# Attention and MoE layer on eight cores: a bf16 input tile cast by the DMA, host-side token order, and the gating split in two

## The reference, cut to what matters

```python
def _L0_attn_ref(x, ...):                  # x: (16, 2048, 1024), SEG = 4, H = 8 heads
    ...                                    # tokens are grouped in segments of SEG = 4
    qk_in = xb @ proj_qk_w.T + proj_qk_b
    v_in = xb @ proj_v_w.T + proj_v_b
    q = (qk_in @ wq.T + bq); k = (qk_in @ wk.T + bk); v = (v_in @ wv.T + bv)
    scores = einsum('nqhd,nkhd->nhqk', q * scale, k)      # 4 x 4 in each segment
    scores = where(diag, finfo.min, scores)
    o = einsum('nhqk,nkhd->nqhd', softmax(scores), v)
    return o @ out_proj_w.T + out_proj_b

def _moe(x, Wg, W1, b1, W2, b2, W3, b3):   # 8 experts, top 2, DFF = 2048
    gout = xt @ Wg.T
    topv, topi = top_k(gout, 2); w = softmax(topv)
    comb = einsum('tke,tk->te', one_hot(topi, E), w)
    h = silu(xt @ W1.T + b1) * (xt @ W2.T + b2)           # every expert on every token
    eo = h @ W3.T + b3
    return einsum('eth,te->th', eo, comb)

x = layernorm(x + attn(x))
x = layernorm(x + moe(x))
```

## Time and profile before

| what | us |
|---|---|
| median of the timed runs (8247.62 to 8254.06) | 8250.84 |
| the profiled execution, its own time | 8323.93 |
| span of its slowest core (the other seven: 8187.3 to 8282.6) | 8322.4 |
| PE busy in that span | 6452.2 |
| VectorE busy | 2236.5 |
| attention phase, from the start to the first load of x1T | about 2131 |

### The profile page before, as it was taken

One profiled execution on the slowest core, in us unless ns is written; L12 is line 12 of the kernel. 1 busy time (PEld: TensorE's weight loads), 2 busy tenths in 40 slices (PEclk: granted clock), 3 DMA queues, 4 the chain that ended last, 5 costly groups with the idle time before them and its releaser, 6 DMA issues.

```text
span 8322.4 us, 79954 instructions; the slowest of 8 cores (8187.3 to 8322.4 us)
## 1 busy us (share of the span) xinstructions
PE 6452.2 (78%) x29024; PEld 2830.4 (34%) x29024; DVE 2236.5 (27%) x3944; ACT 1005.5 (12%) x1621; POOL 309.8 (4%) x591
## 2 busy tenths in 40 slices
PE   4543555335399999938999996699999939999995
PEld 1211222112144444413444442244444414444442
DVE  3334443444222222222222222222222222222111
ACT  0010000100111111111111111111111111111111
POOL 0000000000000000000000000000000000000000
PEclk8766777667699999969999998799999969999886
DMA  4000000000344344432444343234443324334331
GB/s 76 22 26 26 8 19 25 26 25 9 65 72 72 66 77 81 76 81 46 86 76 76 61 91 76 61 66 84 79 76 67 75 72 76 71 64 89 67 65 48
DMA packets 137641, 504.56 MB, mean 61 GB/s; under 512 B 45181, under 2 KB 45310, under 8 KB 127274
## 3 DMA queue, kind: packets, MB, share of 16 engines
q0 software_dynamic: 84080, 415.43, 27.2%
q1 hardware_dynamic: 53178, 84.02, 3.1%
HBM read 872.71 MB, written 41.94 MB: 110 GB/s over the span
## 4 chain that ended last, share of the span: by engine, by line
PE 73%; DVE 12%; DMA 8%; issue 4%; ACT 2%; DVEq 1%; SPq 0%; POOL 0%; ACTq 0%; POOLq 0%
PE pm L830 22%; PE pm L794 20%; PE pm L772 19%; PE pb L385 4%; DMA w2f<-w2T 3%; PE pb L341 3%; DVE ob L480 2%; PE pb L519 2%; DMA x1g<-x1f 2%; DVE Pb L420 1%; DVE Sb L427 1%; DMA X<-x 1%; DVE ob L477 1%; DMA x1T<-x1t 1%; PE pb L394 1%
## 5 line engine op out<-in xcount | busy, mean ns | idle before, releaser
L772 PE MATMUL pm<-x1T,w1f 128*128 128x512 bf16 x8192 | 1969.4, 384 | 28.4 <-DMA w1f<-w1T 21.1
L794 PE MATMUL pm<-x1T,w2f 128*128 128x512 bf16 x8192 | 1962.1, 383 | 11.7 <-DMA w2f<-w2T 11.5
L830 PE MATMUL pm<-w3sb,hsb 128*128 128x512 bf16 x8192 | 1804.3, 384 | 45.0 <-DVE hsb L803 45.0
L803 DVE SCALAR_TENSOR_TENSOR hsb<-pm,b2c_s,su 128x512 bf16<-128x512 f32 x1024 | 769.0, 751 | 2879.6 <-PE pm L772 2550.0
L781 ACT ACTIVATE su<-pm,b1c_s 128x512 bf16<-128x512 f32 x1024 | 705.8, 689 | 4525.5 <-PE pm L772 4447.4
L830 PEld LDWEIGHTS pm<-w3sb,hsb 128*128 128x128 bf16 x8192 | 806.5, 99 | 1042.8 <-issue 161.6
L772 PEld LDWEIGHTS pm<-x1T,w1f 128*128 128x128 bf16 x8192 | 805.1, 99 | 1031.8 <-issue 138.0
L794 PEld LDWEIGHTS pm<-x1T,w2f 128*128 128x128 bf16 x8192 | 806.5, 99 | 1005.7 <-issue 104.0
L843 DVE SCALAR_TENSOR_TENSOR acc<-pm,comb,acc 128x512 f32<-128x512 f32 x512 | 384.4, 751 | 1462.7 <-PE pm L830 1459.7
L497 PE MATMUL trb<-idnb_s,obf 128*128 128x128 bf16 x256 | 32.4, 307 | 706.3 <-DVE obf L488 706.3
L161 POOL DMA_DIRECT2D w1f<-w1T x256 | 135.1, 528 | 6102.8 <-DVE hsb L803 3740.6
(11 more groups left out here) (94 smaller groups left out, 2177.9 us busy)
## 6 DMA issues: line engine op xcount, KB each, us to landing
w1f<-w1T POOLq DMA_DIRECT2D x256, 512.0 KB, 5.3
w2f<-w2T POOLq DMA_DIRECT2D x256, 512.0 KB, 7.3
w3sb<-w3T POOLq DMA_DIRECT2D x64, 2048.0 KB, 22.3
X<-x SPq DMA_DIRECT2D x8, 2048.0 KB, 9.8
x1f<-ob SPq DMA_DIRECT2D x32, 512.0 KB, 2.6
x1g<-x1f SPq DMA_DIRECT2D x32, 512.0 KB, 4.2
out<-outg SPq DMA_DIRECT2D x32, 512.0 KB, 2.9
x1t<-obf SPq DMA_DIRECT2D x32, 256.0 KB, 2.6
```

What stands on the lines that cost most here:

```text
L772: return t.matmul(gb[:, :], w1f[sl % 2][:, kt * 256 + off: kt * 256 + off + 128], x1T[:, kt * MCH + half * 512: kt * MCH + half * 512 + 51 ...
L794: return t.matmul(vb[:, :], w2f[sl % 2][:, kt * 256 + off: kt * 256 + off + 128], x1T[:, kt * MCH + half * 512: kt * MCH + half * 512 + 51 ...
L803: return v.scalar_tensor_tensor(hsb[:, f * MCH + half * 512: f * MCH + half * 512 + 512], vb[:, :], b2c[:, e * 16 + f: e * 16 + f + 1], su ...
L830: return t.matmul(bk[:, :], hsb[:, f * MCH + j * 128: f * MCH + j * 128 + 128], w3sb[:, f * D + half * 512: f * D + half * 512 + 512], sta ...
```

## The change

There are three edits, which come together.

1. The input is permuted on the host so that block i of a chunk is 128 rows in a row (`_vt_perm`), and the output is permuted back on the host; the store of `out` has contiguous rows. `X` (f32) and the two `Xc` tiles go. In their place `Xbf` (bf16, one for all chunks) is loaded on POOL's queue, with the cast done by the DMA, behind the six weights; it is free again after the chunk's last input transpose. The 256 casts of L306 go, and the transposes read `Xbf`.
2. The residual add reads `xres`, two f32 tiles of 128 tokens, each loaded on SP's queue ahead of its block's residual add.
3. The gating of a MoE chunk ends with `comb`. The transpose of `comb`, the copy `combT`, the bias matmuls and the copies into `acc` are a function of their own, `emit_gating_part2`, which is called once for each chunk, after expert 0's hidden stage and before its down-projection.

```diff
-    X = sba("X", [128, 4 * D], F32)
-    Xc = [sba(f"Xc{p}", [128, 128], BF16) for p in range(2)]
+    Xbf = sba("Xbf", [128, 4 * D], BF16)
+    xres = [sba(f"xres{p}", [128, D], F32) for p in range(2)]
...
-        xsrc = bass.AP(x_h.tensor, c * ACH * D, [[SEG * D, 128], [D, 4], [1, D]])
-        t_xl = dma("sync", X[:, :], xsrc, deps=take("X"), sem=ld_X)
+        xsrc = bass.AP(x_h.tensor, c * ACH * D, [[D, 128], [128 * D, 4], [1, D]])
+        t_xl = dma("gpsimd", Xbf[:, :], xsrc, deps=take("Xbf"), sem=ld_X)
...
-            bankdeps = take(bname) + (CONST if c == 0 and i == 0 else [])
+            bankdeps = [t_xl] + take(bname) + (CONST if c == 0 and i == 0 else [])
             ttr = None
             for dt in range(8):
-                t_c = vop(lambda v, s, i=i, dt=dt: v.tensor_copy(
-                    Xc[dt % 2][:, :],
-                    X[:, i * D + dt * 128: i * D + (dt + 1) * 128]),
-                    [t_xl] + take(f"Xc{dt % 2}"))
-
-                def f(t, s, dt=dt, bk=bk):
+                def f(t, s, i=i, dt=dt, bk=bk):
                     return t.transpose(bk[:, dt * 128:(dt + 1) * 128],
-                                       Xc[dt % 2][:, :], idnb[:, :])
-                ttr = top(f, [t_c] + bankdeps)
+                                       Xbf[:, i * D + dt * 128: i * D + (dt + 1) * 128],
+                                       idnb[:, :])
+                ttr = top(f, bankdeps)
                 bankdeps = []
-                use(f"Xc{dt % 2}", ttr)
+            last_tr = ttr
...
+        use("Xbf", last_tr)
...
+            vt0i = c * ACH + i * 128
+            t_xres = dma("sync", xres[par][:, :],
+                         bass.AP(x_h.tensor, vt0i * D, [[D, 128], [1, D]]),
+                         deps=take(f"xres{par}"), sem=ld_xr[par])
...
-                        X[:, i * D + half * 512: i * D + half * 512 + 512],
+                        xres[par][:, half * 512: half * 512 + 512],
                         bk2[:, :], OP.add)
-                tx = vop(fxr, [tmm] + take(f"xr{par}" if half == 0 else "_n"))
+                tx = vop(fxr, [tmm, t_xres]
+                         + take(f"xr{par}" if half == 0 else "_n"))
                 use(bname2, tx)
-                if i == 3 and half == 1:
-                    use("X", tx)
+                use(f"xres{par}", tx)
...
+        def emit_gating_part2():
+            for j in range(8):
+                def ftr(t, s, j=j):
+                    return t.transpose(pm[7][0:8, 0:128],
+                                       comb[:, j * 8:(j + 1) * 8], idnf[:, :])
+                ttr = top(ftr, [comb_tok[j]] + take("pm7"))
...
+            if e == 0:
+                emit_gating_part2()
+
             last_mm = None
             for j in range(8):
...
-            dst = bass.AP(out_h.tensor, (c_ * ACH + i_) * D,
-                          [[SEG * D, 128], [1, D]])
+            dst = bass.AP(out_h.tensor, vt0 * D, [[D, 128], [1, D]])
```

More of the change, by code:

```diff
@@ L133, in build_program @@
     ld_X = P.sem("ld_X")
+    ld_xr = [P.sem("ld_xr0"), P.sem("ld_xr1")]
     ld_x1T = P.sem("ld_x1T")
@@ L294, in build_program @@
     for c in range(N_ACH):
-        xsrc = bass.AP(x_h.tensor, c * ACH * D, [[SEG * D, 128], [D, 4], [1, D]])
-        t_xl = dma("sync", X[:, :], xsrc, deps=take("X"), sem=ld_X)
+        xsrc = bass.AP(x_h.tensor, c * ACH * D, [[D, 128], [128 * D, 4], [1, D]])
+        t_xl = dma("gpsimd", Xbf[:, :], xsrc, deps=take("Xbf"), sem=ld_X)
         xT_evacs = []
         xT_guard = take("xT")
+        last_tr = None
         for i in range(4):
@@ L325, in build_program @@
             xT_evacs.append(tev)
+        use("Xbf", last_tr)
         if DEBUG_TAPS and c == 0:
-            use("X", dma("sync", dbg["dbg_X"], X[:, :], deps=[t_xl], sem=st_dbgs["dbg_X"]))
             use("xT", dma("sync", dbg["dbg_xT"], xT[:, :], deps=xT_evacs,
@@ L532, in build_program, with fxr @@
                 use(f"oT{par}", tmm)
-                def fxr(v, s, par=par, half=half, bk2=bk2, i=i):
+                def fxr(v, s, par=par, half=half, bk2=bk2):
                     return v.tensor_tensor(
                         xr[par][:, half * 512: half * 512 + 512],
-                        X[:, i * D + half * 512: i * D + half * 512 + 512],
+                        xres[par][:, half * 512: half * 512 + 512],
                         bk2[:, :], OP.add)
-                tx = vop(fxr, [tmm] + take(f"xr{par}" if half == 0 else "_n"))
+                tx = vop(fxr, [tmm, t_xres]
+                         + take(f"xr{par}" if half == 0 else "_n"))
                 use(bname2, tx)
-                if i == 3 and half == 1:
-                    use("X", tx)
+                use(f"xres{par}", tx)
                 xr_parts.append(tx)
@@ L702, in build_program @@
             comb_tok[j] = t_cb
[L704 to L730, removed]
@@ new lines, in emit_gating_part2, with fce, fmm, fai @@
+        def emit_gating_part2():
[4 more added lines that the diff above has]
+                ttr = top(ftr, [comb_tok[j]] + take("pm7"))
+                def fce(v, s, j=j):
+                    return v.tensor_copy(combT[:, j * 128:(j + 1) * 128],
+                                         pm[7][0:8, 0:128])
+                t_ct = vop(fce, [ttr] + take(f"combTg{j}"))
+                use("pm7", t_ct)
+                for half in range(2):
+                    bn = f"pm{half}"
+                    def fmm(t, s, j=j, half=half):
+                        return t.matmul(pm[half][:, :],
+                                        combT[:, j * 128:(j + 1) * 128],
+                                        b3s[:, half * 512: half * 512 + 512],
+                                        start=True, stop=True)
+                    tmm2 = top(fmm, [t_ct] + take(bn))
+                    use(f"combTg{j}", tmm2)
+                    def fai(v, s, j=j, half=half):
+                        return v.tensor_copy(
+                            acc[:, j * D + half * 512: j * D + half * 512 + 512],
+                            pm[half][:, :])
+                    t_ai = vop(fai, [tmm2] + take(f"accg{j}{half}"))
+                    use(bn, t_ai)
+                    acc_tok[(j, half)] = t_ai
@@ L888, in build_program @@
             use(f"xr2{par}", t_o)
-            c_ = g // 4
-            i_ = g % 4
-            dst = bass.AP(out_h.tensor, (c_ * ACH + i_) * D,
-                          [[SEG * D, 128], [1, D]])
+            dst = bass.AP(out_h.tensor, vt0 * D, [[D, 128], [1, D]])
             t_st = dma("sync", dst, outg[par][:, :], deps=[t_o], sem=st_o[par])
@@ L975, in _host_prep, with _vt_perm @@
     }
+def _vt_perm():
+    p = np.empty(T, dtype=np.int64)
+    for c in range(N_ACH):
+        for i in range(4):
+            for n in range(128):
+                p[c * 512 + i * 128 + n] = c * 512 + 4 * n + i
+    return p
 def kernel(**inputs):
@@ L981 @@
     xs = x.reshape(N_CORES, 2 * 2048, D)
+    perm = _vt_perm()
     in_maps = []
@@ L984 @@
         m = dict(com)
-        m["x"] = np.ascontiguousarray(xs[c])
+        m["x"] = np.ascontiguousarray(xs[c][perm])
         in_maps.append(m)
@@ L988 @@
     res = run_bass_kernel_spmd(nc, in_maps, core_ids=list(range(N_CORES)))
-    out = np.concatenate([np.asarray(r["out"]).reshape(2, 2048, D)
-                          for r in res.results], axis=0)
-    return out.astype(np.float32)
+    outs = []
+    for r in res.results:
+        ov = np.asarray(r["out"])
+        oreal = np.empty_like(ov)
+        oreal[perm] = ov
+        outs.append(oreal.reshape(2, 2048, D))
+    return np.concatenate(outs, axis=0).astype(np.float32)
 if __name__ == "__main__":
```

## The result

The changed kernel takes 0.9818 of the time of the kernel before, with a 95% interval of 0.9798 to 0.9837: **1.8% less**. The forecast was 8101 us against 8250.84, a ratio of 0.982. The executions of the changed kernel that the ratio rests on took 8090 to 8134 us, all but one of them 8090 to 8100. What follows reads core 5 in both profiles. The first fence shows two cores of the changed kernel, with span and mean granted clock; the second is core 5 of the kernel before.

The account below looks back on a forecast made before the run. The chain was 73% PE, mostly MoE matmuls left unchanged; the change touches stretches where PE stands. Terms -162.4, +48.8 and -36 sum to -149.6 us, giving 8101 us from 8250.84, range 8080 to 8125, whole range 8055 to 8150.

Parts of the forecast that it names:

- the one from the sum to the chances: Turning the forecast time into chances: 0.24 for over 2% faster, 0.74 for within 2%, 0.02 for over 2% slower.
- The sum: Whole kernel: -162.4 at boundaries, +48.8 at the start, -36 for the gating split, together -149.6 us.
- the middle of expert 0: Between expert 0's hidden stage and down-projection: the moved gating rounds delay the down-projection, a loss of 21.8 us per MoE chunk.
- the cold restart: Expert 0's down-projection in each MoE chunk starts at the lower clock after the wait, costing 1.8 us.
- The boundary: Between attention chunks: copy to projection takes 5.1 us instead of 28.3, saving 23.2 at each of 7, 162.4 in all.
- The cold start that I left in: First projection matmuls of each attention chunk: a 2.2 us slow-clock cost assumed to stay, gain 0, at most 15 us.
- the rival that had it going: Cold start goes at 7 boundaries (15 us), Xbf lands at 84 (6), acc rounds faster (10): 181 us, 8070; chance 0.2.
- The first chunk: Program start: Xbf queues behind six weights, lands at 90.4, projection starts at 95.5; a loss of 48.8 us, between 42 and 60.
- xres: Residual add in attention: its 32 loads land in 4.2 us with 18.9 us of slack, cost 0.
- the rival that had it late: Residual add waits for xres: at a slow load's pace 822 us more, 8923 us; chance 0.02.
- The gating: MoE chunks: head gains 32.5 us, middle loses 21.8, cold start 1.8; net 8.9 each, 36 us for four.
- The rival that had it worthless: Gating split gives nothing if rounds in expert 0 take 3.9 us: 8137, or 8149 with Xbf landing at 102; chance 0.13.

Follow-up runs that it names:

- Xbf held back: The changed kernel with each next Xbf load held until the last copy of the chunk before; fastest time 8169 us, 77 us more than the changed kernel.
- the doubled transposes: The changed kernel with each of a chunk's 32 input transposes issued twice; fastest time 8099.38 us, 7 us more than the changed kernel, measured once.

## Why the prediction was right, and where it wasn't

**The step that failed is the one from the sum to the chances.** The prediction says "About 2% is what a measurement of this kernel can tell from no change", and so puts 0.74 on a time within 2%, as if 1.8% were no clear change. The record had the number against it: the timed runs of the kernel before, 8247.62 to 8254.06, lie within 0.08% of each other. The interval of the measurement is 0.4% wide (0.9798 to 0.9837), and no change, 1.0, stands far outside it. The sum said 150 us, and the bounds of its terms (137 for the boundaries, 60 for the first chunk, 0 for the gating split) leave a gain of 77 us even all together. What I should have drawn from it is that a gain was near certain, and only its being over or under 2% open; that stays open even now, for 0.98 lies inside the interval.

**The time and its direction were right**, with 1.8% forecast and 1.8% measured, and each mechanism of the sum was there. That the total came within 6 us of core 5's is in part luck: the boundaries gave 17 us more than their term, and the start, the middle of expert 0 and the cold restart together cost 12 us more than theirs.

- *The boundary.* The four rounds of 5.1 us are there, to 0.1 us. The term was the most mis-sized: 179.3 measured for 162.4. From the end of the last copy to the projection the seven boundaries took 203.1 us on core 5 before (29.0 each, where the one that I read had 28.3) and 35.1 after, a gain of 168.0. The wait for X is part of that: 103.0 less 24.0 at the start leaves 79.0, or 11.3 each, where I had 10.7. Another 6.4 us came from the projection that starts each of the seven stretches, which is the cold start, below. The last 5.0 lie in the four blocks of a chunk, and nothing here says why.
- *The cold start that I left in.* The step "I leave it in: the transposes of before do not clear it, and the new ones are denser but last only 5 us" failed. The projection's first matmuls gained 7.6 us over the 8 chunks. What I held against the rival that had it going, that TensorE rests before each of these places as much as before, was wrong too: at the boundary shown it was idle 13.5 us before the first transpose, and is now idle 1.0. That rest is not what decides, though: with Xbf held back it was 12 to 14 us again, and the clock still rose at 2 of the 7. The Trainium skill ("TensorE: Matmul & The Clock Gate", part 4) says that transposes don't count as busy for the clock gate; the doubled transposes disagree with it, with 111.9 us where the rule would leave 119 or more. The bound of 15 us was the right way to think of it, and half of it came.
- *The first chunk.* The loss was 54.7 where I took 48.8. The first transpose is at 91.8, against a forecast landing of 90.4, and the projection at 96.8 for 95.5. The rest is the base: on core 5 the kernel before started at 42.1 rather than at 46.7, because its first cast could start at 24.0 rather than at 28.65. Moving the load proves the cause: the queue, not the cast and not the 4 KB rows.
- *xres.* Cost 0, as forecast; the rival that had it late is out. It landed in 4.1 to 5.6 us, where 18.9 were free.
- *The gating.* Head -32.6 a chunk (forecast -32.5), middle +22.5 (+21.8), cold restart +2.6 (+1.8), together -30 us for -36, and both runs that do or undo the split alone say 29 to 33. The rival that had it worthless is out.

Not settled: the 3.2 us less between the last projection and the first gating, of which the eighth projection's own faster start is 1.4, the 5.0 us in the blocks, and the +2.1 of the rest. Parts of a MoE chunk that no edit touches differ by several us between runs of the same code (the first MoE chunk, from gating to gating on core 5, took 1532.4 us in the changed kernel and 1522.3 in the one with Xbf held back, which is the same there), so I would not read anything into them. The store of `out` with contiguous rows has no run of its own; its median landing is 2.9 us in both profiles.

## What to carry to other kernels

A preload moved to another queue takes that queue's place in line: 55 us were lost at the start for a load that takes 12 at the head of the queue, and moving one issue gave 61 back. Work moved off one critical place is only gained if it lands where another engine is busy: the gating's second half was first moved (30 us for the whole split), then spread between matmul groups (another 63 to 82 us). Where eight small chains waited for one PSUM bank, writing all of them into columns of that bank and working once on the wide tile removed the waits between them (23.0 us to 1.7) and most of the small operations.

## What was not expected of the hardware

Transposes raised TensorE's clock. With 64 transposes ahead of it the first projection ran at full clock in every chunk (111.9 us for 512 matmuls); with 32 in quick succession it did in part (119.1, the granted clock above 0.50 at 4 boundaries of 7; from 2 to 4 of 7 on other cores and in other runs of the same code, such as 2 with 121.1 us on core 6); with 32 drawn out over 17 us by the casts it took 126.7, and the clock stood at 0.50 at all seven. The casting load of 1 MB as written landed 84 us after its issue behind six weights, and had a median of 9.4 over the eight chunks; where something waited for it, it took 12.2 and 12.6 us from issue to the first transpose.
